# Cross-attention scores of one token tile by four row tiles into four PSUM banks, and a new order of the steps around them

## The chip, the cores and the metric

The kernel runs on one core of one Trainium2 chip. The metric is the device time of one execution in microseconds (us). A measurement of this kernel tells a change of about 1% from none.

## The reference, cut to what matters

The reference is one decoder layer on 2 x 1024 tokens of 256 values: causal self-attention with 16 heads of 16, cross-attention on 64 context rows, and a mixture of 16 experts (top 4) with a shared expert, each followed by an added residual and a layer norm. The change is in the cross-attention:

```python
q = split_heads(queries @ Wq + bq)
k = split_heads(keys @ Wk + bk)
v = split_heads(values @ Wv + bv)
scores = jnp.einsum('bhqd,bhkd->bhqk', q, k) / jnp.sqrt(jnp.float32(HD))
scores = jnp.where(mask, jnp.float32(-1000000000000000.0), scores)
attn = jax.nn.softmax(scores, axis=-1)
ctx = jnp.einsum('bhqk,bhkd->bhqd', attn, v)
...
return ctx @ Wo + bo
```

Here `HD` is 16 and there are 16 heads, so one token has 16 x 64 scores. A tile of 128 tokens has 128 x 1024 scores, which is two PSUM banks of 512 columns.

## The kernel before, in words

The program has three long stretches: the self-attention (to about 300 us of the profiled span), the cross-attention with the routing to experts (354 us to about 517 us), and 79 blocks of expert work (to about 690 us). The change touches the second.

The 2048 tokens are 16 tiles of 128. `x_order()` writes out a list `XO` of (kind, n) from the table `LAGS`, and every engine walks through this one list in its order and does the kinds that it has work for. A **step** is one pass over the table; two steps make one token tile, because kinds S, T and V come once for each half of the heads (n = 2 x tile + half). A kind with lag k handles in step s the index n = s - k. Kinds whose n must be odd come once in two steps. The kinds are:

- S: TensorE multiplies queries and keys of 8 heads into a bank and adds the mask through an identity matrix (L1643, L1645). VectorE takes the maximum over each head (L1239) and subtracts it (L1243, semaphore `xs_sub`). ScalarE takes the exponential (L833, `xp_exp`).
- T: TensorE turns the probabilities by four 128x128 transposes (L1652), ScalarE copies them out of PSUM (L840, `xpT_kept`).
- V: TensorE multiplies them with the values (L1662, `xo_ready`). The value matrix has a column of ones, so that the row sums come along.
- N, once per tile: VectorE takes the reciprocal of the sums (L1252) and scales (L1254, `xo_norm`).
- P and O: TensorE turns the context (L1672), ScalarE copies it (L846, `xo_kept`).
- Y: TensorE multiplies by the output weights (L1679, `y_ready`); VectorE adds the residual and makes the statistics of the layer norm (`norm_stats`, L990 to L996), GpSimd takes the power (L708).
- Z and X: the norm is applied by VectorE (L1039) and ScalarE (L850), TensorE turns the tile back (L1545), ScalarE copies it (L854).
- L, R, Q, W, K, I: once for each group of four tiles, the router. After I, GpSimd scatters the rows of the group to the experts' slots, 16 indirect DMAs of kind C (L738), three in a step.

All engines but TensorE's weight loads keep strictly to this order. In PSUM, banks 0 and 1 hold the scores of an even and an odd n, banks 2 and 3 the transposes of an even and an odd n, bank 4 the values of all 16 heads, bank 5 the turned context and the router's ranks, bank 6 the output product, bank 7 the turned tile and the router's logits. An S needs the subtraction two n back, a T the copy two n back.

## Time and profile before

| what | value |
|---|---|
| median of 3 runs | 711.37 us (708.14 to 714.35) |
| the profiled execution's own time | 716.99 us |
| its span in the trace | 715.3 us |
| TensorE busy over the span | 610.7 us (85%) |
| VectorE busy over the span | 469.3 us (66%) |
| ScalarE, GpSimd busy | 351.5 us (49%), 316.6 us (44%) |
| first and last score matmul (L1643) | 354.5 us, 457.8 us |

Busy is time in which an engine has an instruction in it. TensorE's matmuls overlap in the pipeline, so the time from one matmul's start to the next one's start, not the duration of one, is what it costs the engine.

### The profile page before, as it was taken

To read this page: it belongs to the slowest core of one execution; us is meant where nothing else is said; L and a number is where in the kernel's file an instruction comes from. 1 tells how busy PE (TensorE), PEld (TensorE's weight loads), DVE (VectorE), ACT (ScalarE), POOL (GpSimd) and SP (SyncE) were. 2 spreads that over 40 slices of the span, in tenths; PEclk is the share of its full clock that TensorE was granted. 3 is DMA by queue.
4 is the path that set the end of the run, shared out by engine and by line. 5 is a ranking of instruction groups with operands and counts; after the bars stand their busy time and mean duration, and the time that the engine had idled before them with its cause. 6 is when DMAs were issued, how large, how long until landed. Compare 5 with 4: busy or idle time off the path is not lost.

```text
span 715.3 us, 12852 instructions
## 1 busy us (share of the span) xinstructions
PE 610.7 (85%) x3820; PEld 369.4 (52%) x3820; DVE 469.3 (66%) x1304; ACT 351.5 (49%) x735; POOL 316.6 (44%) x393
## 2 busy tenths in 40 slices
PE   5888899999999998998799997958646888888884
PEld 3434434434434342254377774834436777777741
DVE  0369878888788883069478874736325756767657
ACT  1312376666676667816375442413223545555543
POOL 8413312234332442547666163545474454554530
PEclk9989999999999999999999996979867999999988
DMA  5867766337165300049000021111354664566756
GB/s 165 169 169 148 159 211 93 67 50 99 30 80 81 44 4 18 18 146 372 1 1 0 1 73 56 64 64 57 120 160 142 201 203 138 152 208 198 240 200 212
DMA packets 52113, 82.51 MB, mean 115 GB/s; under 512 B 11936, under 2 KB 29600, under 8 KB 51744
## 3 DMA queue, kind: packets, MB, share of 16 engines
q1 hardware_dynamic: 45184, 62.26, 35.6%
q0 software_dynamic: 6864, 19.44, 7.4%
q8 instruction: 34, 0.56, 0.3%
q14 instruction: 31, 0.25, 0.1%
HBM read 53.38 MB, written 32.48 MB: 120 GB/s over the span
## 4 chain that ended last, share of the span: by engine, by line
PE 62%; DVE 17%; another core or an unknown queue 6%; ACT 4%; issue 4%; DMA 3%; POOL 2%; SPq 1%; DVEq 0%; ACTq 0%; POOLq 0%
PE ps L1480 9%; PE ps L1745 9%; PE ps L1456 8%; PE ps L1439 7%; DVE neg_max L922 5%; PE ps L1768 4%; PE ps L1643 3%; PE ps L1662 3%; PE ps L1724 2%; PE ps L1788 2%; PE ps L1757 2%; PE ps L1588 2%; PE ps L1444 2%; PE ps L1652 2%
## 5 line engine op out<-in xcount | busy, mean ns | idle before, releaser
L922 DVE TENSOR_REDUCE neg_max<-ps 128x1 f32<-128x512 f32 (+3 forms) x304 | 181.9, 655 | 43.1 <-PE ps L1444 26.6
L775 ACT ACTIVATE temps<-ps 128x1024 f32<-128x1024 f32 (+1 forms) x192 | 147.5, 812 | 78.1 <-PE ps L1456 78.0
L674 POOL TENSOR_SCALAR_AFFINE_SELECT temps<-temps 128x256 f32<-128x256 f32 x128 | 52.2, 411 | 148.1 <-ACT temps L775 147.2
L1439 PE MATMUL ps<-stacks 96*128 96x512 bf16 (+3 forms) x384 | 105.4, 331 | 11.6 <-DMA stacks<-qk_parts 5.1
L745 POOL DMA_INDIRECT expert_outputs<-x_T,w_o_xqkv x79 | 76.6, 970 | 74.3 <-ACT x_T L895 37.5
L1456 PE MATMUL ps<-stacks 99*128 99x512 bf16 (+3 forms) x384 | 93.3, 328 | 2.9 <-DMA stacks<-m_rows 1.4
L1480 PE MATMUL ps<-temps,v_group 128*32 128x512 f32 (+3 forms) x768 | 81.8, 497 | 1.6 <-POOL temps L674 1.0
L1745 PE MATMUL ps<-w_split,block_x 128*128 x474 | 73.0, 291 | 5.8 <-DVE block_x L1327 2.9
L738 POOL DMA_INDIRECT expert_slots<-x_tok,w_o_xqkv x64 | 62.4, 974 | 28.7 <-issue 17.2
L1745 PEld LDWEIGHTS ps<-w_split,block_x 128*128 128x128 f32 x474 | 64.2, 196 | 7.4 <-issue 7.2
L1456 PEld LDWEIGHTS ps<-stacks 99*128 99x128 bf16 x384 | 26.9, 97 | 75.1 <-ACT temps L775 49.6
L1439 PEld LDWEIGHTS ps<-stacks 96*128 96x128 bf16 x384 | 37.3, 98 | 49.2 <-DVE neg_max L922 20.7
L882 ACT ACTIVATE o_norm<-ps 128x128 f32<-128x128 f32 x79 | 22.4, 283 | 60.9 <-PE ps L1745 45.0
L708 POOL TENSOR_TENSOR ln_rstd<-ln_var_eps,minus_half 128x1 f32<-128x1 f32 x32 | 18.8, 588 | 73.8 <-DVE ln_var_eps L996 73.8
L1349 DVE TENSOR_TENSOR o_norm<-ps,o_norm 128x128 f32<-128x128 f32 x79 | 22.6, 286 | 43.7 <-ACT o_norm L882 33.2
L1444 PE MATMUL ps<-caus_a,ident_b 128*128 128x128 bf16 x256 | 50.7, 224 | 0.0
L1768 PE MATMUL ps<-w_split,block_h 128*128 x237 | 50.0, 320 | 0.1
L1757 PE MATMUL ps<-ident_f,o_norm 128*128 128x128 f32 x79 | 23.7, 300 | 29.6 <-DVE o_norm L1349 20.7
L833 ACT ACTIVATE o_norm<-o_norm 128x512 f32<-128x512 f32 x32 | 20.2, 630 | 48.4 <-DVE o_norm L1243 45.7
L1327 DVE TENSOR_TENSOR block_x<-ps,block_x 128x256 fp32r<-128x256 f32 x79 | 33.1, 420 | 11.1 <-ACT block_x L874 6.5
L1494 PE MATMUL ps<-x_T,w_qkv 128*128 128x512 f32 x64 | 32.0, 642 | 7.5 <-DMA x_T<-in_xT 7.5
L874 ACT ACTIVATE block_x<-ps 128x256 fp32r<-128x256 f32 x79 | 31.0, 392 | 14.2 <-PE ps L1724 10.4
(213 smaller groups left out, 1092.6 us busy)
## 6 DMA issues: line engine op xcount, KB each, us to landing
stacks<-qk_parts SPq DMA_DIRECT2D x96, 128.0 KB, 5.7
v_group<-expert_slots SPq DMA_DIRECT2D x79, 138.5 KB
qk_parts<-temps SPq DMA_DIRECT2D x8, 768.0 KB, 4.4
w_raw<-in_w SPq DMA_DIRECT2D x4, 1024.0 KB, 10.4
early_parts<-expert_outputs SPq DMA_DIRECT2D x4, 1024.0 KB
expert_slots<-in_pad SPq DMA_DIRECT2D x16, 138.5 KB
expert_slots<-in_pad SPq DMA_DIRECT2D x1, 2077.5 KB
x_T<-in_xT SPq DMA_DIRECT2D x4, 512.0 KB, 7.4
```

Of the source, the lines that this page charges most:

```text
L674: nc.gpsimd.affine_select(diag, diag, [[0, 2], [1, P]], ALU.is_ge, zero, base=0, channel_multiplier=-1).then_inc(b_cut, 1)
L738: pool.indirect_dma_start(slots, bass.IndirectOffsetOnAxis(ridx[:, t, k:k + 1].bitcast(U32), 0), xe[:, t, :], None).then_inc(scattered[q], 16)
L745: pool.indirect_dma_start(sums_of, bass.IndirectOffsetOnAxis(idxs[:, b:b + 1].bitcast(U32), 0), yb[:, b % YB, :], None).then_inc(landed[b ...
L775: nc.scalar.activation(pt[:, n % 4, :, 0:w], ps[:, 2 + 2 * (n % 2):4 + 2 * (n % 2), 0:w], ACT.Exp, scale=SCALE).then_inc(b_exp, 1)
L922: nc.vector.tensor_reduce(nmx[:, c, h0:h0 + nh, i], ps[:, A_BANKS[n % 3], 0:w * nh].rearrange("p (h k) -> p h k", h=nh), axis=AX.X, op=ALU ...
L1439: last = nc.tensor.matmul(ps[:, A_BANKS[n % 3], w * s:w * s + w], qs[0:KR, ua, h0 + s, P * i:P * i + P], ks[0:KR, ua, h0 + s, CH * c:CH * ...
L1444: last = nc.tensor.matmul(ps[:, A_BANKS[n % 3], w * (s + 1) - P:w * (s + 1)], identb[:], causA[:], start=False, stop=True)
L1456: last = nc.tensor.matmul(ps[:, bank, 0:w], ks[0:KM, u, 2 * pr + s, P * j:P * j + P], qs[0:KM, u, 2 * pr + s, q0:q0 + w], start=True, stop ...
L1480: last = nc.tensor.matmul(ps[HS * h:HS * h + HS, 6, CH - w:CH], vg[:, u, j, h, :], pt[:, (2 * p + h // 2) % 4, h % 2, 0:w], start=(j == 0) ...
L1745: last = nc.tensor.matmul(ps[:, 2 + b % 2, 0:D], xsp[b % 3][:, xp, k, :], w13s[:, bass.ds(expert[b], 1), wp, at:at + 2 * INTER], start=(k ...
L1757: nc.tensor.transpose(ps[:, 4 + b % 2, 0:P], hblk[:, b % 3, :], identf[:]).then_inc(hb_T, 1)
L1768: last = nc.tensor.matmul(ps[:, 6 + b % 2, 0:D], hsp[:, b % 3, hp, :], w2s[:, bass.ds(expert[b], 1), wp, :], start=(n == 0), stop=(n == 2))
```

## The change

Scores: instead of one product of 128 query rows with a block-diagonal key matrix for each half of the heads, the S of an even n makes the scores of the whole tile, and the S of an odd n makes nothing on TensorE. Each group of 32 rows of the array (two heads) is a tile of its own with 128 key columns, and its scores go to bank q. Four mask matmuls of 256 columns replace two of 512. All four score banks are taken by one token tile, so that the S of an even n waits for both subtractions of the tile before. Transposes keep one bank (4), so that each T waits for the copy of the T before. The values of the two halves go to banks 5 and 6, behind columns 0 to 255. Kind Y now stands ahead of V in the table; its work on VectorE stays where it was and is now kind F.

```diff
-LAGS = {"S": 0, "T": 2, "V": 4, "N": 4, "P": 5, "O": 5, "Y": 6, "Z": 7, "X": 8, "L": 9, "R": 9, "Q": 10,
+LAGS = {"S": 0, "T": 2, "Y": 6, "V": 4, "N": 4, "P": 5, "O": 5, "F": 6, "Z": 7, "X": 8, "L": 9, "R": 9, "Q": 10,
         "W": 11, "K": 12, "I": 12}
...
-                    nc.scalar.activation(pTx[:, n % 2].rearrange("p r s -> p (r s)"), ps[:, 2 + n % 2, :],
+                    nc.scalar.activation(pTx[:, n % 2].rearrange("p r s -> p (r s)"), ps[:, 4, :],
...
                 if kind == "S":
-                    s3 = ps[:, n % 2, :].rearrange("p (h k) -> p h k", h=8)
-                    dve.wait_ge(xs_ready, n + 1)
-                    nc.vector.tensor_reduce(mxx[:, n % 2, :], s3, axis=AX.X, op=ALU.max).then_inc(xs_max, 1)
+                    s4 = ps[:, 0:4, P * (n % 2):P * (n % 2) + P].rearrange("p q (h k) -> p q h k", h=2)
+                    m3 = mxx[:, n % 2, :].rearrange("p (q h) -> p q h", h=2)
+                    dve.wait_ge(xs_ready, n // 2 + 1)
+                    nc.vector.tensor_reduce(m3, s4, axis=AX.X, op=ALU.max).then_inc(xs_max, 1)
...
                 if kind == "N":
-                    heads = ps[:, 4, 0:H * VW].rearrange("p (h v) -> p h v", h=H)
+                    heads = ps[:, 5:7, D:D + H // 2 * VW].rearrange("p o (h v) -> p o h v", v=VW)
                     dve.wait_ge(xo_ready, 2 * n + 2)
+                    wait(dve, xo_kept, n)
...
-                if kind == "Y":
+                if kind == "F":
                     dve.wait_ge(y_ready, NT + n + 1)
...
                 if kind == "S":
-                    t, o = n // 2, n % 2
-                    if n >= 2:
-                        pe.wait_ge(xs_sub, n - 1)
-                    nc.tensor.matmul(ps[:, n % 2, :], q2[:, o, P * t:P * t + P],
-                                     kbd[:, o, t // TB].rearrange("p h k -> p (h k)"), start=True, stop=False)
-                    nc.tensor.matmul(ps[:, n % 2, :], identb[:], mask[:, t, :].unsqueeze(1).to_broadcast([P, 8, S2]),
-                                     start=False, stop=True).then_inc(xs_ready, 1)
+                    if n % 2 == 0:
+                        t = n // 2
+                        wait(pe, xs_sub, n)
+                        for o in range(2):
+                            for q in range(4):
+                                rows = slice(32 * q, 32 * q + 32)
+                                nc.tensor.matmul(ps[:, q, P * o:P * o + P], q2[rows, o, P * t:P * t + P],
+                                                 kbd[rows, o, t // TB, 2 * q:2 * q + 2].rearrange("p h k -> p (h k)"),
+                                                 start=(o == 0), stop=False, skip_group_check=True)
+                        for q in range(4):
+                            last = nc.tensor.matmul(ps[:, q, 0:2 * P], identb[:],
+                                                    mask[:, t, :].unsqueeze(1).to_broadcast([P, 4, S2]),
+                                                    start=False, stop=True, skip_group_check=True)
+                        last.then_inc(xs_ready, 1)
                 if kind == "T":
                     pe.wait_ge(xp_exp, n + 1)
-                    if n >= 2:
-                        pe.wait_ge(xpT_kept, n - 1)
+                    wait(pe, xpT_kept, n)
...
                     pe.wait_ge(xpT_kept, n + 1)
-                    if o == 0 and t >= 1:
-                        pe.wait_ge(xo_norm, t)
+                    if o == 0:
+                        wait(pe, xo_norm, t)
+                        wait(pe, xo_kept, oT_turned[0])
+                        wait(pe, r_index, ranked[0])
+                    else:
+                        taken[0] = t + 1
```

TensorE's order for one token tile of the steady stretch before the change is this (v_group is the key or value matrix, o_norm the queries, probabilities or context, according to the line):

```order
L1643 MATMUL ps<-v_group,o_norm 128x512
L1645 MATMUL ps<-w_qkv,ident_b 128x512
L1652 MATMUL ps<-ident_f,o_norm 128x128 x4
L1662 MATMUL ps<-v_group,o_norm 128x34 x4
L1672 MATMUL ps<-ident_f,o_norm 128x128 x2
L1643 MATMUL ps<-v_group,o_norm 128x512
L1645 MATMUL ps<-w_qkv,ident_b 128x512
L1652 MATMUL ps<-ident_f,o_norm 128x128 x4
L1662 MATMUL ps<-v_group,o_norm 128x34 x4
L1679 MATMUL ps<-w_xo,o_norm 128x256 x2
L1545 MATMUL ps<-ident_f,x_tok 128x128 x2
```

After the change TensorE's order for one token tile of the same stretch is this:

```order
L1650 MATMUL ps<-v_group,o_norm 128x128 x8
L1654 MATMUL ps<-w_qkv,ident_b 128x256 x4
L1662 MATMUL ps<-ident_f,o_norm 128x128 x4
L1676 MATMUL ps<-v_group,o_norm 128x34 x4
L1686 MATMUL ps<-ident_f,o_norm 128x128 x2
L1662 MATMUL ps<-ident_f,o_norm 128x128 x4
L1693 MATMUL ps<-w_xo,o_norm 128x256 x2
L1676 MATMUL ps<-v_group,o_norm 128x34 x4
L1550 MATMUL ps<-ident_f,x_tok 128x128 x2
```

The scores have moved to the front of the tile as one piece, no score work stands between the first P (L1686) and the second T (L1662), and the output product Y (L1693) now stands ahead of the second V (L1676).

VectorE's order for one token tile after the change, with what each instruction waits for, is this:

```order
L1241 TENSOR_REDUCE x_max<-ps 128x8 [waits xs_ready]
L1245 TENSOR_TENSOR o_norm<-ps,x_max 128x512 [waits xp_exp,xs_max]
L1040 SCALAR_TENSOR_TENSOR ln_minus_mean<-ln_mean_var,ln_rstd 128x1 [waits ln_pow]
L1241 TENSOR_REDUCE x_max<-ps 128x8 [waits xs_ready]
L1245 TENSOR_TENSOR o_norm<-ps,x_max 128x512 [waits xp_exp,xs_max]
L1256 RECIPROCAL x_rsum<-ps 128x16 [waits xo_norm,xoT_ready,xo_kept,xo_ready]
L1258 TENSOR_TENSOR o_norm<-ps,x_rsum 128x256 [waits xo_recip]
L991 TENSOR_TENSOR x_tok<-ps,x_tok 128x256 [waits ln_done,bo_added,y_ready]
L993 BN_STATS ln_stats<-x_tok 128x6 [waits ln_in]
L995 BN_AGGR ln_mean_var<-ln_stats 128x2 [waits ln_chain]
L997 TENSOR_SCALAR ln_var_eps<-ln_mean_var 128x1 [waits ln_chain]
```

Before the change VectorE had the same instructions in the same order; only the wait for `xo_kept` ahead of the reciprocal is new. ScalarE's order is unchanged too.

## Rows read from the trace of the kernel before

**Rows 1.** The page's busy time of each engine.
```profile
PE 610.7 (85%) x3820; PEld 369.4 (52%) x3820; DVE 469.3 (66%) x1304; ACT 351.5 (49%) x735; POOL 316.6 (44%) x393
```

**Rows 2.** Timeline of TensorE, one tile: start us, us, engine, line, operation, [idle before].
```profile
383.27 1.02 PE L1643 MATMUL ps<-v_group,o_norm 128*128 128x512 f32 x2
384.13 0.38 PE L1645 MATMUL ps<-w_qkv,ident_b 128*128 128x512 bf16 x1
384.34 0.60 PE L1652 MATMUL ps<-ident_f,o_norm 128*128 128x128 f32 x4
384.78 0.98 PE L1662 MATMUL ps<-v_group,o_norm 128*128 128x34 f32 x8
385.59 0.41 PE L1672 MATMUL ps<-ident_f,o_norm 128*128 128x128 f32 x2
...
388.17 1.11 PE L1679 MATMUL ps<-w_xo,o_norm 128*128 128x256 f32 x4
389.12 0.38 PE L1545 MATMUL ps<-ident_f,x_tok 128*128 128x128 f32 x2
389.33 1.02 PE L1643 MATMUL ps<-v_group,o_norm 128*128 128x512 f32 x2
```

**Rows 3.** Timeline of VectorE and ScalarE in the same tile.
```profile
384.54 0.69 DVE L1239 TENSOR_REDUCE x_max<-ps 128x8 f32<-128x512 f32 x1
385.27 0.69 DVE L1243 TENSOR_TENSOR o_norm<-ps,x_max 128x512 f32<-128x512 f32 x1
...
386.00 0.63 ACT L833 ACTIVATE o_norm<-o_norm 128x512 f32<-128x512 f32 x1 [2.10 <-DVE o_norm L1243]
...
386.53 0.58 ACT L840 ACTIVATE o_norm<-ps 128x512 f32<-128x512 f32 x1
...
388.45 0.25 DVE L1252 RECIPROCAL x_rsum<-ps 128x16 f32<-128x16 f32 x1
...
388.74 0.42 DVE L1254 TENSOR_TENSOR o_norm<-ps,x_rsum 128x256 f32<-128x256 f32 x1
...
389.32 0.42 DVE L990 TENSOR_TENSOR x_tok<-ps,x_tok 128x256 f32<-128x256 f32 x1 [0.16 <-PE ps L1679]
...
389.78 0.43 DVE L992 BATCH_NORM_STATS2 ln_stats<-x_tok 128x6 f32<-128x256 f32 x1
...
390.45 0.15 DVE L996 TENSOR_SCALAR ln_var_eps<-ln_mean_var 128x1 f32<-128x1 f32 x1
390.61 0.69 DVE L1239 TENSOR_REDUCE x_max<-ps 128x8 f32<-128x512 f32 x1
```

**Rows 4.** Timeline of TensorE, scores of the first three tiles.
```profile
354.51 1.10 PE L1643 MATMUL ps<-v_group,o_norm 128*128 128x512 f32 x2 [0.98 <-ACT o_norm L814]
...
357.34 1.13 PE L1643 MATMUL ps<-v_group,o_norm 128*128 128x512 f32 x2 [0.44 <-DVE o_norm L1243]
...
360.47 1.02 PE L1643 MATMUL ps<-v_group,o_norm 128*128 128x512 f32 x2
```

**Rows 5.** Timeline of TensorE, self-attention products on four column tiles of 32.
```profile
120.48 0.43 PE L1480 MATMUL ps<-temps,v_group 128*32 128x128 f32 x8
...
122.70 1.06 PE L1480 MATMUL ps<-temps,v_group 128*32 128x512 f32 x8
```

**Rows 6.** Timeline: first scatter of two groups, and the ScalarE instruction after the stall.
```profile
414.42 1.20 POOL L738 DMA_INDIRECT expert_slots<-x_tok,w_o_xqkv  x1 [0.67 <-DVE w_o_xqkv L1107]
...
437.48 0.22 ACT L860 ACTIVATE w_o_xqkv<-ps 128x64 f32<-128x64 f32 x1 [5.79 <-remote]
...
451.49 1.04 POOL L738 DMA_INDIRECT expert_slots<-x_tok,w_o_xqkv  x1 [0.83 <-DVE w_o_xqkv L1107]
...
473.86 0.22 ACT L860 ACTIVATE w_o_xqkv<-ps 128x64 f32<-128x64 f32 x1 [6.50 <-remote]
```

**Rows 7.** Windows: us, busy PE, PEld, DVE, ACT, POOL, granted clock, DMA, GB/s.
```profile
588.00:595.00 7.00, 5.77 (x46) 5.30 (x45) 3.94 (x16) 3.32 (x14) 3.13 (x4) 1.00 0.53 162
```

**Rows 8.** Timeline of TensorE, values product at the lower clock.
```profile
441.29 1.76 PE L1662 MATMUL ps<-v_group,o_norm 128*128 128x34 f32 x8
```

More of the change, by code:

```diff
@@ L162, in x_order @@
                     out.append((kind, n))
-            elif kind in "NPOYZX":
+            elif kind in "NPOYFZX":
                 if n % 2 and 0 < n < 2 * NT:
@@ L563, in _ @@
             sp.wait_ge(kv_kept, 20)
-            sp.wait_ge(xs_ready, 2 * NT)
+            sp.wait_ge(xs_ready, NT)
             sp.wait_ge(bo_added, NT)
@@ L1251, in _ @@
                         dve.wait_ge(xoT_ready, n - 1)
-                    nc.vector.reciprocal(rsx[:, n % 2, :], heads[:, :, DH]).then_inc(xo_recip, 1)
+                    sums = rsx[:, n % 2, :].rearrange("p (o h) -> p o h", o=2)
+                    nc.vector.reciprocal(sums, heads[:, :, :, DH]).then_inc(xo_recip, 1)
                     dve.wait_ge(xo_recip, n + 1)
-                    nc.vector.tensor_tensor(ox[:, n % 2, :].rearrange("p (h v) -> p h v", h=H), heads[:, :, 0:DH],
-                                            rsx[:, n % 2, :].unsqueeze(2).to_broadcast([P, H, DH]),
+                    nc.vector.tensor_tensor(ox[:, n % 2, :].rearrange("p (o h v) -> p o h v", o=2, v=DH),
+                                            heads[:, :, :, 0:DH],
+                                            sums.unsqueeze(3).to_broadcast([P, 2, H // 2, DH]),
                                             ALU.mult).then_inc(xo_norm, 1)
-                if kind == "Y":
+                if kind == "F":
                     dve.wait_ge(y_ready, NT + n + 1)
@@ L1575, in project @@
             def project(c, part):
-                if c < 2 and part == 0:
-                    pe.wait_ge(xs_sub, 2 * NT - 1 + c)
-                if c < 2 and part == 1:
-                    pe.wait_ge(xpT_kept, 2 * NT - 1 + c)
+                if c < 2:
+                    pe.wait_ge(xs_sub, 2 * NT)
                 if c >= 2:
@@ L1611, in ranks @@
                 pe.wait_ge(xo_kept, oT_turned[0])
+                pe.wait_ge(xo_norm, taken[0])
                 if q >= EARLY:
@@ L1626, in ranks @@
                 if q >= 1:
-                    last = nc.tensor.matmul(ps[:, 5, D + GMAX * E:D + (GMAX + 1) * E], ones, msum[:, q], start=True,
+                    last = nc.tensor.matmul(ps[:, 5, RANK + GMAX * E:RANK + (GMAX + 1) * E], ones, msum[:, q], start=True,
                                             stop=True)
@@ L1639, in _ @@
                 if kind == "S":
-                    t, o = n // 2, n % 2
-                    if n >= 2:
-                        pe.wait_ge(xs_sub, n - 1)
-                    nc.tensor.matmul(ps[:, n % 2, :], q2[:, o, P * t:P * t + P],
-                                     kbd[:, o, t // TB].rearrange("p h k -> p (h k)"), start=True, stop=False)
-                    nc.tensor.matmul(ps[:, n % 2, :], identb[:], mask[:, t, :].unsqueeze(1).to_broadcast([P, 8, S2]),
-                                     start=False, stop=True).then_inc(xs_ready, 1)
+                    if n % 2 == 0:
[12 more added lines that the diff above has]
+                        last.then_inc(xs_ready, 1)
                 if kind == "T":
                     pe.wait_ge(xp_exp, n + 1)
-                    if n >= 2:
-                        pe.wait_ge(xpT_kept, n - 1)
+                    wait(pe, xpT_kept, n)
                     for r in range(4):
-                        last = nc.tensor.transpose(ps[:, 2 + n % 2, P * r:P * r + P], px[:, n % 2, P * r:P * r + P],
+                        last = nc.tensor.transpose(ps[:, 4, P * r:P * r + P], px[:, n % 2, P * r:P * r + P],
                                                    identf[:])
@@ L1657, in _ @@
                     pe.wait_ge(xpT_kept, n + 1)
-                    if o == 0 and t >= 1:
-                        pe.wait_ge(xo_norm, t)
+                    if o == 0:
[4 more added lines that the diff above has]
+                        taken[0] = t + 1
                     for r in range(4):
-                        at = 2 * VW * (4 * o + r)
-                        last = nc.tensor.matmul(ps[:, 4, at:at + 2 * VW], pTx[:, n % 2, r, :],
+                        at = D + 2 * VW * r
+                        last = nc.tensor.matmul(ps[:, 5 + o, at:at + 2 * VW], pTx[:, n % 2, r, :],
                                                 vbd[:, t // TB, 4 * o + r, :], start=True, stop=True)
@@ L1753, in _ @@
                     elif b == 0:
-                        pe.wait_ge(xo_norm, NT)
+                        pe.wait_ge(xpT_kept, 2 * NT)
                     else:
```

13 lines of the change are left out of this document (7 added, 6 removed).

## The prediction

> **What bounds the kernel now.** I began with the busy shares of the page, where TensorE stands first with 85% [rows 1]. A share over the whole span says little on one stage, so I went to the timeline of TensorE in the cross-attention. There a token tile costs 389.33 - 383.27 = 6.06 us from one even score product to the next, and each row of TensorE begins where the one before it lets go: two halves of scores 0.86, mask 0.21, transposes 0.44, values 0.81, P 0.25, Y 0.95, X 0.21 [rows 2]. That is 2 x (0.86 + 0.21 + 0.44 + 0.81) + 0.25 + 0.95 + 0.21 = 6.05 us with no gap. So in the steady stretch TensorE is full, and the others wait for it: VectorE's F stood 0.16 us for Y, and ScalarE 2.10 us for the subtraction [rows 3]. The reader should see a second thing in the same rows. ScalarE took the exponential at 386.00, right behind the subtraction, and only then the copy of a transpose that TensorE had finished at 384.94 [rows 2, 3]. In list order the copy of T(n-2) stands behind the exponential of S(n). Before the change this lateness costs nothing, since TensorE has a second transpose bank and a second score product to do meanwhile.
>
> **What it removes from TensorE.** A row tile of 32 appears nowhere in this trace; the nearest rows are the products on four column tiles of 32. Eight of them with 128 columns take 0.43 us together, 0.27 to issue and 0.16 to drain [rows 5]; one after another they would need 8 x 0.11, by the transposes' 0.44 for four [rows 2]. Both halves of the new scores are 16 such instructions in the trace (two passes of f32 each), so 2 x 0.27 plus a drain of 0.16 ahead of the masks, which stand in the full array; the masks are 4 x 256 columns, as many as before, 0.43, and the last ends 0.17 later. The scores of a tile are then ready 1.30 us after they start. Upper bounds: one after another 16 x 0.11 + 0.16 + 0.43 + 0.17 = 2.5; with every weight load exposed too, at the 0.10 us a load that the eight value products show [rows 2], 4.1. Lower bound 1.1, without the drain. I take 1.30, for rows 5 overlap fully and differ only in which side of the array is split. TensorE's work in a tile falls from 6.05 to 3.91 + 1.2 = 5.1 us.
>
> **What it adds: waits, in a ring.** Three things move at once. The second T of a tile waits for the copy of the first, which on ScalarE stands behind the exponential of the first half. Y stands ahead of the second V. And the second V is what N on VectorE waits for, with F and the next tile's maximum queued behind N. Followed from VectorE's first maximum of a tile: maximum and subtraction 1.42 (384.54 to 385.96), handover 0.04, exponential until the copy may start 0.53, copy 0.58 (to 387.11) [rows 3], handover to TensorE 0.05, second T 0.44, Y 0.95, second V until its end 0.98 [rows 2], handover 0.03, then N and F 390.61 - 388.45 - 0.16 = 2.00 until the next maximum may start [rows 3]. The sum is 1.42 + 0.04 + 0.53 + 0.58 + 0.05 + 0.44 + 0.95 + 0.98 + 0.03 + 2.00 = **7.02 us a tile**, against 6.06 now: +0.96. TensorE's own side of the ring, from scores ready to scores ready, is 1.42 + 0.04 + 0.53 + 0.58 + 0.05 + 0.44 + 0.95 + 0.81 + 0.21 + 1.30 = 6.33, so it is not what ends last; it would be if the scores took over 2.0 us. What is behind the waiting T on TensorE is Y, V, X and the next scores, and all of VectorE's N and F wait with them. The wait of N for `xo_kept` costs nothing: that copy is of the tile before and lies some 2 us earlier. The waits of the even V lie on copies a tile old, and the wait of SyncE is now for half the count with the same end; the two new waits at the shared expert and at the first expert block are for work long done. All of this is zero. VectorE's operands over two or four banks have as many elements as before, and I take 0.69 us [rows 3] for each.
>
> **The sum over the stretch.** Start: with one set of score banks the next scores wait for both subtractions, 1.30 + 2 x 1.42 + 0.1 = 4.24 us a tile, where the first two tiles now take 2.83 and 3.13 [rows 4]: +2.5. From there to the first scatter are 8 tiles, 8 x 0.96 = 7.7, less 0.7 for those in which the pipeline is not yet full: the first scatter starts 9.5 us later. From the first scatter of a group to the router's next ScalarE instruction pass 23.06 and 22.37 us, far more than 2.5 tiles need, with ScalarE idle for 5.79 and 6.50 us before it [rows 6]. These stretches go by the scatter's pace, and I let them hide half of 2.5 x 0.96: +1.2 each. Between them 1.5 tiles: +1.4. Behind the second, with the last score work done, +0.5. Together 9.5 + 1.2 + 1.4 + 1.2 + 0.5 = **+13.8 us**. The routing tables and the expert blocks hang on this chain and start that much later; nothing in them changes. On the profiled execution's own time that is 716.99 + 13.8 = 730.8; that execution lies 5.6 us above the median of the runs, and against the median 711.37 it is 725.2. I forecast 725 us. A 1% step, 7.1 us, is about what a measurement of this kernel can tell from no change.
>
> **Rivals.**
> (a) The row tiles don't run side by side, so the change doesn't do what it says. For it: no row of this trace shows a row tile, and 16 weight loads of 128 columns must find room where 4 did. Against it: rows 5. With 2.5 us the ring through TensorE is 5.03 + 2.5 = 7.53, +1.47 a tile. Start +4.9, 8 tiles +11.8 less 0.8, then 1.8 + 2.2 + 1.8 + 0.6: +22, 734 us. With exposed loads, 4.1 us, the tile takes 9.1 and the kernel some 42 us more, 753.
> (b) Faster, by one mechanism: the ring does not close. If the copy, Y or N of one tile could run beside the members that I put behind them, only engine work would be left, 5.1 us on TensorE, with VectorE at 2 x 1.42 + 2.00 = 4.84 beside it [rows 3]. Then 11.5 tiles gain 0.96 each, less the 2.5 of the start: -8.5, 703 us. It decides at 6.06: of the 7.02 some 0.96 would have to go, as much as Y alone. All its members stand in program order on their engines or wait by semaphore, which leaves it little. The Trainium skill, TensorEngine Tiling (Array Packing), section PSUM Bottleneck, names the copies out of PSUM as what may bound once TensorE is four times faster; read as busy time, that is this case, a gain up to VectorE's bound, while the rows above speak for the order of the waits and a loss.
> (c) The stalls of rows 6 fall elsewhere. ScalarE's 5.79 and 6.50 us wait for something that no engine releases, while indirect DMAs run. If one of them lies under other waits in the slower kernel, some 6 us come back: 719; with both, 713.
> (d) The clock. TensorE would be busy 5.1 of 7.02 us with a gap of some 2 us in each tile. A window with 5.77 of 7 busy has the clock at 1.00 throughout [rows 7]. At half the clock the values product takes 1.76 instead of 0.98 [rows 2, 8], so T, Y and V would add 1.9 us to the ring. If half of the tiles ran so, +13 more: 738. The Trainium skill, TensorE: Matmul & The Clock Gate, section A second HAM failure mode, tells of short idle times between groups of matmuls that make the clock fall back and forth; by that rule this rival would be the likely one, by rows 7 it is not.
>
> **How the numbers follow.** The ring with overlapping row tiles 0.62 (718 to 732 us, for the start, the hidden share and the drain are each uncertain by a few us), (a) 0.15 at 734 and 0.03 at 753, (c) 0.10 at 713 to 719, (d) 0.05 at 738, (b) 0.05 at 703. The range reaches from 715, which takes in the upper half of (c), to 737, which takes in the cheaper (a); left out are (b), the lower part of (c), (d) and the dear end of (a), under 2 in 10. Over 1% slower means above 718.5: all of (a) and (d), nearly all of the first, a little of (c), 0.85. Within 1%: 0.10. Faster: 0.05.
>
> **What would show it.** The score groups of 128x128 should stand with their eight entries a half in about 0.4 us, and the masks end 1.3 us after the first score. TensorE should be idle for some 1 to 2 us ahead of the second T of each tile, released by ScalarE's copy. VectorE should be idle ahead of the reciprocal, released by the values product. Even score products should stand 7.0 us apart between the tiles 5 and 9, and the first scatter should start near 9.5 us later against the first score. The distance from first scatter to the next router instruction should be near 23 to 25 us. The forecast is wrong if the distance of the tiles is under 6.1 us (the ring does not close) or over 7.5 us with long score groups (the row tiles don't overlap).

## The result, and the profile after

The changed kernel took 734.64 us (median of 4 runs, 733.30 to 745.80), the kernel before 712.86 us beside it (median of 4, 708.14 to 719.04). The ratio is **1.032, 95% interval 1.025 to 1.040**, or +23 us (+17.5 to +28.4). An execution over 1.5% above the fastest of its kernel goes into no ratio in this document, here 745.80 and 719.04 us. The profiled execution took 733.3 us with a span of 731.6, 16.3 above the span of before.

The page, busy times and the clock over 40 slices, against [rows 1]:

```profile
PE 612.7 (84%) x4044; PEld 383.2 (52%) x4044; DVE 469.1 (64%) x1304; ACT 353.6 (48%) x735; POOL 317.7 (43%) x393
...
PEclk9989899999999999999759978697975999999998
```

The clock row of before:

```profile
PEclk9989999999999999999999996979867999999988
```

The busy times are within 14 us of what they were, and say nothing of where 16 us went. The clock rows say something. In the stretch that the change touches, digits of 5 to 8 now begin with the twentieth slice (348 us); before they began with the twenty-fifth (429 us), behind the first scatter.

TensorE's timeline over one steady tile, against [rows 2]:

```profile
390.22 0.73 PE L1650 MATMUL ps<-v_group,o_norm 32*128 32x128 f32 x16
390.88 0.61 PE L1654 MATMUL ps<-w_qkv,ident_b 128*128 128x256 bf16 x4
391.33 0.60 PE L1662 MATMUL ps<-ident_f,o_norm 128*128 128x128 f32 x4
391.76 0.98 PE L1676 MATMUL ps<-v_group,o_norm 128*128 128x34 f32 x8
392.58 0.42 PE L1686 MATMUL ps<-ident_f,o_norm 128*128 128x128 f32 x2
394.61 0.63 PE L1662 MATMUL ps<-ident_f,o_norm 128*128 128x128 f32 x4 [1.62 <-ACT o_norm L841]
395.07 1.03 PE L1693 MATMUL ps<-w_xo,o_norm 128*128 128x256 f32 x4
395.94 0.98 PE L1676 MATMUL ps<-v_group,o_norm 128*128 128x34 f32 x8
396.75 0.42 PE L1550 MATMUL ps<-ident_f,x_tok 128*128 128x128 f32 x2
397.10 0.73 PE L1650 MATMUL ps<-v_group,o_norm 32*128 32x128 f32 x16
```

A tile takes 397.10 - 390.22 = 6.88 us. From the first of the sixteen products on row tiles to the next row pass 0.66 us, so they overlap. The second T waits 1.62 us for ScalarE's copy (L841).

VectorE and ScalarE in the same tile, against [rows 3]:

```profile
391.91 0.68 DVE L1241 TENSOR_REDUCE x_max<-ps 128x8 f32<-128x512 f32 x1
392.62 0.69 DVE L1245 TENSOR_TENSOR o_norm<-ps,x_max 128x512 f32<-128x512 f32 x1
...
396.95 0.26 DVE L1256 RECIPROCAL x_rsum<-ps 128x16 f32<-128x16 f32 x1 [1.79 <-PE ps L1676]
...
398.94 0.68 DVE L1241 TENSOR_REDUCE x_max<-ps 128x8 f32<-128x512 f32 x1
```
```profile
393.35 0.63 ACT L834 ACTIVATE o_norm<-o_norm 128x512 f32<-128x512 f32 x1 [2.34 <-DVE o_norm L1245]
393.89 0.58 ACT L841 ACTIVATE o_norm<-ps 128x512 f32<-128x512 f32 x1
```

Here is the ring, link by link: maximum at 391.91, subtraction, exponential at 393.35, copy at 393.89, second T at 394.61, Y, second V at 395.94, reciprocal at 396.95, maximum of the next tile at 398.94.

The same in the waits view of 356 to 490 us (total, times, longest):

```profile
ACT o_norm L834 <- DVE o_norm L1245: 55.6, 21, 6.3
DVE x_rsum L1256 <- PE ps L1676: 27.7, 12, 4.8
PE ps L1662 <- ACT o_norm L841: 22.8, 14, 5.2
```

Three engines wait for one another in a circle, and none of them is full.

The scores of the first tiles, against [rows 4], with two waits of transposes:

```profile
356.96 0.73 PE L1650 MATMUL ps<-v_group,o_norm 32*128 32x128 f32 x16 [0.98 <-ACT o_norm L815]
...
361.06 0.73 PE L1650 MATMUL ps<-v_group,o_norm 32*128 32x128 f32 x16 [2.83 <-DVE o_norm L1245]
...
365.33 1.09 PE L1662 MATMUL ps<-ident_f,o_norm 128*128 128x128 f32 x4 [1.89 <-ACT o_norm L841]
366.35 1.24 PE L1650 MATMUL ps<-v_group,o_norm 32*128 32x128 f32 x16
...
424.45 1.08 PE L1662 MATMUL ps<-ident_f,o_norm 128*128 128x128 f32 x4 [2.75 <-ACT o_norm L841]
```

The second tile comes 4.10 us behind the first (4.24 in the sum). In the third tile, and in the two behind it, the same sixteen products take 1.24 us instead of 0.73: that is the clock. Windows of the start (us, busy PE, PEld, DVE, ACT, POOL, granted clock, DMA, GB/s):

```profile
361.00:368.00 7.00, 5.04 (x47) 3.79 (x48) 2.68 (x5) 4.06 (x9) 7.00 (x9) 0.57 0.00 0
...
375.00:382.00 7.00, 6.64 (x29) 5.91 (x28) 2.67 (x4) 2.96 (x6) 0.00 (x0) 0.50 0.01 2
382.00:389.00 7.00, 6.23 (x46) 5.46 (x47) 4.83 (x11) 3.01 (x6) 3.84 (x5) 0.73 0.00 0
389.00:396.00 7.00, 5.38 (x56) 4.72 (x54) 4.88 (x11) 3.47 (x8) 3.66 (x5) 1.00 0.01 2
...
424.00:431.00 7.00, 6.12 (x39) 5.29 (x39) 4.90 (x17) 2.57 (x6) 0.18 (x1) 0.50 0.00 0
```

A 0.50 is TensorE at 1.2 GHz, a 1.00 at 2.4. Behind the 2.83 us of waiting ahead of the second tile the engine is low for most of 28 us. A busy share read alone would mislead here: 6.64 of 7 us busy, since each instruction lasts longer. In the steady tiles of this trace, with a gap of 1.62 to 1.77 us in each, the clock is full. From 424 us on, behind a wait of 2.75 us, it is at 0.50 again.

The scatters and the router, against [rows 6]:

```profile
432.04 1.20 POOL L739 DMA_INDIRECT expert_slots<-x_tok,w_o_xqkv  x1 [0.67 <-DVE w_o_xqkv L1108]
...
457.29 0.22 ACT L861 ACTIVATE w_o_xqkv<-ps 128x64 f32<-128x64 f32 x1 [2.09 <-remote]
...
473.57 1.04 POOL L739 DMA_INDIRECT expert_slots<-x_tok,w_o_xqkv  x1 [0.83 <-DVE w_o_xqkv L1108]
...
494.23 0.22 ACT L861 ACTIVATE w_o_xqkv<-ps 128x64 f32<-128x64 f32 x1 [3.47 <-remote]
```

Cut at the first scores and the first scatter of each of the four groups, the two executions differ so: first scores +2.5 us, to the first scatter 75.1 instead of 59.9 (+15.2), to the second 41.5 instead of 37.1 (+4.4), to the third +2.2, to the fourth +0.2, from there to the end -8.2. Of the last piece 4.5 us lie among the 79 expert blocks (from the first to the last scatter of their outputs 145.3 us before and 140.9 here), which the change leaves as they were, and 3.3 us behind them, where TensorE's granted clock was 0.79 before (687 to 701 us) and 1.00 here (711 to 717 us). ScalarE's waits that no engine releases lie elsewhere, between the scatters: 5.79 and 6.50 us ahead of the router's instruction in [rows 6], 2.09 and 3.47 here. With the other waits of that kind between the same scatters they come to 10.7 and 11.3 us before, 7.5 and 8.4 here. The execution of before was 5.6 us above the median of the runs that the forecast went by, that of after 1.3 below its own.

### The profile page after: what moved, and what is told of

It is laid out like the page before. It is cut to its first block, busy times and chain, and to the rows that moved or that the text cites. A ratio compares the mean times of both kernels' runs of the same rounds, so it can differ in the third digit from the quotient of the medians.

```text
span 731.6 us, 13325 instructions
## 1 busy us (share of the span) xinstructions
PE 612.7 (84%) x4044; PEld 383.2 (52%) x4044; DVE 469.1 (64%) x1304; ACT 353.6 (48%) x735; POOL 317.7 (43%) x393
## 3 DMA queue, kind: packets, MB, share of 16 engines
q1 hardware_dynamic: 45184, 62.26, 34.8%
## 4 chain that ended last, share of the span: by engine, by line
PE 54%; DVE 19%; DMA 6%; issue 6%; ACT 5%; another core or an unknown queue 4%; POOL 2%; SPq 2%; DVEq 0%; ACTq 0%; POOLq 0%
PE ps L1485 9%; PE ps L1461 8%; PE ps L1444 7%; PE ps L1759 7%; DVE neg_max L923 5%; PE ps L1782 3%; PE ps L1676 2%; DMA v_group<-expert_slots 2%; PE ps L1693 2%; PE ps L1738 2%; PE ps L1449 2%; PE ps L1591 2%; DVE x_max L1241 2%; PE ps L1662 2%
## 5 line engine op out<-in xcount | busy, mean ns | idle before, releaser
L1444 PE MATMUL ps<-stacks 96*128 96x512 bf16 (+3 forms) x384 | 106.8, 336 | 10.7 <-DMA stacks<-qk_parts 4.9
L739 POOL DMA_INDIRECT expert_slots<-x_tok,w_o_xqkv x64 | 62.3, 974 | 28.7 <-issue 17.2
L883 ACT ACTIVATE o_norm<-ps 128x128 f32<-128x128 f32 x79 | 22.3, 282 | 53.7 <-PE ps L1759 37.4
L1662 PE MATMUL ps<-ident_f,o_norm 128*128 128x128 f32 x128 | 24.9, 328 | 23.6 <-ACT o_norm L841 22.8
L1771 PE MATMUL ps<-ident_f,o_norm 128*128 128x128 f32 x79 | 23.6, 299 | 22.7 <-DVE o_norm L1354 19.4
L1676 PEld LDWEIGHTS ps<-v_group,o_norm 128*128 128x128 f32 x256 | 39.2, 227 | 6.0 <-ACT o_norm L841 4.7
L1676 PE MATMUL ps<-v_group,o_norm 128*128 128x34 f32 x256 | 37.4, 297 | 4.5 <-ACT o_norm L841 4.5
```

Source lines behind the costliest of these rows:

```text
L739: pool.indirect_dma_start(slots, bass.IndirectOffsetOnAxis(ridx[:, t, k:k + 1].bitcast(U32), 0), xe[:, t, :], None).then_inc(scattered[q], 16)
L1444: last = nc.tensor.matmul(ps[:, A_BANKS[n % 3], w * s:w * s + w], qs[0:KR, ua, h0 + s, P * i:P * i + P], ks[0:KR, ua, h0 + s, CH * c:CH * ...
L1676: last = nc.tensor.matmul(ps[:, 5 + o, at:at + 2 * VW], pTx[:, n % 2, r, :], vbd[:, t // TB, 4 * o + r, :], start=True, stop=True)
```

## The experiments

They ran in groups on several chips, each beside the kernel before on the same chip. In three groups the kernel before takes 656 to 658 us, in the other two groups, the result's and the last, 710 to 713. So only differences and ratios are compared. "Stretches" are the times from the first scores to the first scatter, and from scatter to scatter.

### The changed kernel and the kernel before on a quicker chip

Both unmodified.

> The changed kernel, unmodified, beside the three that follow on one chip. The ring theory (a tile of a tail lasts 6.88 us against 6.06, and the clock falls while the pipeline fills) does not lean on the long idle stretches of the first trace: the steps are the same on any chip, so the difference in us stays, +18 to +24 over the kernel before, and the granted clock is again 0.5 to 0.75 in the first 30 us behind the first scores. The rival, that part of the difference came from where those idle stretches fall, gives less than +14 on a chip where they are absent.

> The kernel before, unmodified, for its trace on the kind of chip where it takes some 656 us. A steady tile 6.06 us, the sixth tile's scores 22.7 us behind the first, and the first scatter about 60 us behind, all as in the first trace, since none of this leans on where it ran. The rival, that the tails themselves differ from chip to chip, gives other values for these three.

Measured: changed kernel 684.98 us median (677.51 to 689.40, 4 runs) beside 657.67, profiled at 681.63 with a span of 679.7. Of the four, 677.51 and 681.63 us count for a ratio, which is about 1.034. Before, on another chip of the quicker kind: 658.77 us, span 657.0. The difference of the spans is 22.7 us. In the trace of before a tile is 6.07 us, the sixth tile comes 22.7 us behind the first, the first scatter 59.9: the tails are the same on both kinds of chip. For the changed kernel these are 6.88 (one tile, from 386.85 us), 32.2 and 77.4. Windows of the changed kernel from its first scores on, and then of before:

```profile
354.00:390.00 36.00, 25.90 (x228) 22.04 (x228) 18.92 (x38) 15.64 (x32) 17.97 (x25) 0.81 0.00 1
390.00:432.00 42.00, 34.62 (x268) 29.96 (x269) 27.64 (x86) 17.00 (x36) 11.53 (x16) 0.77 0.01 2
```
```profile
354.00:377.00 23.00, 22.57 (x125) 15.38 (x126) 17.09 (x32) 14.48 (x30) 15.99 (x21) 1.00 0.01 1
377.00:414.00 37.00, 35.27 (x228) 27.11 (x227) 30.52 (x92) 16.66 (x37) 13.03 (x19) 0.99 0.00 1
```

Here the clock fell in the steady tiles too. At 398.26 us TensorE came out of the ring's own wait, and the two tiles that begin at 393.73 and 401.98 us took 8.25 and 8.99 us:

```profile
398.26 0.63 PE L1662 MATMUL ps<-ident_f,o_norm 128*128 128x128 f32 x4 [1.76 <-ACT o_norm L841]
```
```profile
399.00:409.00 10.00, 9.64 (x54) 8.28 (x53) 5.42 (x11) 3.87 (x8) 4.24 (x6) 0.52 0.00 0
```

In the first trace the same wait, 1.77 us, ended at 401.63 us, and the clock stayed at 1.00.

The stretches differ by +17.5, +2.9, +3.3 and +1.0 us, the start by +0.7, the rest behind the last scatter by -2.8. That last piece is again the work behind the expert blocks, at a clock of 0.79 before (635 to 643 us) and 1.00 for the changed kernel (659 to 666 us). What differs between the chips is ScalarE's wait: the router's instruction (L860) has no idle time before it here.

```profile
429.86 0.20 ACT L860 ACTIVATE w_o_xqkv<-ps 128x64 f32<-128x64 f32 x1
```

So the loss does not hang on where those stalls fall. The first scores' +2.5 us of the first trace are +0.7 here and lie ahead of everything that the change touches.

### One part alone in the kernel before: Y ahead of V

```diff
-LAGS = {"S": 0, "T": 2, "V": 4, "N": 4, "P": 5, "O": 5, "Y": 6, "Z": 7, ...
+LAGS = {"S": 0, "T": 2, "Y": 6, "V": 4, "N": 4, "P": 5, "O": 5, "F": 6, "Z": 7, ...
```

> The kernel before with kind Y ahead of V in the table (its VectorE part as kind F in the old place), nothing else; banks and scores as before. My theory, the ring of waits: Y waits for ScalarE's copy O, which stands behind the exponential and the transposes' copy, and now V and with it N wait behind Y. Members by the rows of before: N and F 2.00, maximum and subtraction 1.42, exponential 0.53, copy 0.58, O 0.38, Y 0.95, V 0.98 with handovers 0.1: 6.9 us a tile instead of 6.06, so some 7 to 9 us more in all, although TensorE has all its old work. Rival: TensorE is full at 6.05 us a tile and its work is only reordered, so the time stays within 2 us of before.

Measured: 665.69 us, ratio 1.016 (1.013 to 1.019). Scores, masks and banks are those of before. The tile grew to 390.31 - 383.62 = 6.69 us (6.9 expected), with one gap:

```profile
388.28 1.13 PE L1679 MATMUL ps<-w_xo,o_norm 128*128 128x256 f32 x4 [0.41 <-ACT o_norm L846]
```

Y now waits for ScalarE's copy O (L846), and V stands behind it, though V's own data are there. The first stretch grew by 3.4 us. The clock stayed at 1.00 in every window from 353 to 460 us: the order of Y alone costs, without any help from the clock.

### One part alone in the kernel before: one bank for the transposes

```diff
-                    if n >= 2:
-                        pe.wait_ge(xpT_kept, n - 1)
+                    wait(pe, xpT_kept, n)
-    transpose(ps[:, 2 + n % 2, P * r:P * r + P], ...)
+    transpose(ps[:, 2, P * r:P * r + P], ...)
```

> The kernel before with one bank for the transposes instead of two, nothing else. Theory of the prediction, that the second T waits for the copy behind the exponential: here a score product of 1.07 us stands between, so T reaches its turn 2.57 us after the scores and the copy is done at about 2.6: 6.1 to 6.4 us a tile, and 1 to 2 us in the start; 2 to 7 us more in all. Rival: the single bank alone makes the whole loss, 7.0 us a tile and some 14 us more.

Measured: 666.49 us, ratio 1.017 (1.013 to 1.022), a tile of 6.43 us, the first stretch 65.6 instead of 59.9. The gap ahead of T is short, 0.17 us by L840, because the score products of the second half stand between the two T and cover the copy. In the changed kernel these have moved to the head of the tile. The tile is near the expected 6.1 to 6.4 us, the loss of 10.4 us is above the expected 2 to 7: the first stretch holds 5.6 of it, and where the rest lies was not found. The start of this kernel has gaps too, TensorE is busy for 3.67 us from 360 to 366 us, and there the clock stayed at 1.00. Each part alone costs about 10 us, and both together with the single set of score banks 22.7.

### The ring cut at its ScalarE link

In the changed kernel, ScalarE gets a list XA of its own, in which T (in the second kernel T and O) stands ahead of S in each step, and so the copy of the transposes ahead of the exponential:

```diff
-            for kind, n in XO:
+            for kind, n in XA:
```

> The changed kernel, but ScalarE does the copy of the transposes ahead of the exponential in each step. Theory: exponential and copy leave the ring at the second T; what is left is the ring through O and Y, without the copy: 6.3 us a tile instead of 6.88, so 5 to 8 us less than the changed kernel. Rival: the clock or VectorE decides, and the time stays within 2 us of the changed kernel. Second rival: the exponentials come later by the copy and the tile gets longer.

> The changed kernel, but ScalarE does both the copy of the transposes and the copy O of the turned context ahead of the exponential. Theory: both rings through ScalarE open, and TensorE's 5.1 us, VectorE's 4.9 us and what is left of handovers decide: 5.4 to 5.8 us a tile, 10 to 14 us less than the changed kernel, about the time of the kernel before (the start still costs 2 to 9 us). Rival: as for the run with the copy alone ahead, if O is no member, 6.3 us a tile.

Measured: copy ahead 675.46 us, ratio 1.033 (1.026 to 1.040), tile 6.21 to 6.36 us. Copy and O ahead 669.37 us, ratio 1.023 (1.015 to 1.030), tile 5.85 us. TensorE in the second of them:

```profile
386.52 0.63 PE L1663 MATMUL ps<-ident_f,o_norm 128*128 128x128 f32 x4 [0.59 <-ACT o_norm L842]
```

The wait of the second T fell from 1.62 to 0.59 us and the tile by 1.03, below the 6.07 of before. The link is shown. The times followed less well than the tiles. With the copy alone ahead the ratio is that of the changed kernel (1.032 and about 1.034), where 5 to 8 us less were expected, and with both copies the kernel is still 2% slower than before, where about the time of before was expected: what is left of the loss does not lie in the steady tile. In the window from 360 to 366 us its clock was 0.50.

### The same order on ScalarE in the kernel before

XA has T and O ahead of S again.

```diff
-            for kind, n in XO:
+            for kind, n in XA:
```

> The kernel before with ScalarE's copy of the transposes and O ahead of the exponentials, which took 1.03 us off a tile of the changed kernel. With two banks for the transposes and two for the scores no ring closes through ScalarE there, and VectorE's and TensorE's rows set the tile: 6.0 us, the same time within 2 us. The rival, that the order on ScalarE was costing the kernel before as well, gives a tile below 5.9 and 3 to 8 us less.

Measured: 657.36 us beside 656.67, ratio 1.001 (0.997 to 1.005), tile 6.07 us. Where two banks hide the lateness of the copy, its place in the list is worth nothing that shows. No version came out ahead of the kernel before.

### A member of the ring made shorter

```diff
-                    for o in range(2):
+                    for o in range(1):
                         last = nc.tensor.matmul(ps[:, 6, 0:D], oTx[:, n % 2, o, :], wxo[:, o, :], ...
```

> The changed kernel with one of the two matmuls of each output projection Y left out, so half of the attention's heads do not reach the result. This shortens Y by about half of its 0.95 us. If Y lies on the ring of waits, a steady tile shrinks from 6.88 to 6.4 or 6.5 us and the time by 6 to 9 us; if the ring closes beside Y, as the rival has it, TensorE idles longer where Y was, and both stay.

Measured: **686.20 us beside 656.67, ratio 1.045** (1.037 to 1.054). The tile shrank as expected, to 6.54 us on the average of four (378.68 to 404.85): Y is on the ring. The first stretch shrank too, from 77.4 us on the quicker chip to 70.7. The time did not; with less to do for TensorE the kernel is no faster than the changed one, in the ratio even above its 1.032. The windows of the second and the third stretch:

```profile
424.00:462.00 38.00, 36.47 (x226) 31.64 (x225) 22.79 (x77) 13.85 (x29) 18.24 (x21) 0.54 0.17 61
462.00:500.00 38.00, 35.77 (x165) 29.47 (x164) 17.26 (x67) 12.55 (x25) 18.10 (x21) 0.57 0.18 61
```

The second and third stretch last 37.4 and 37.9 us, 4.5 and 7.4 more than in the changed kernel on the quicker chip, at a clock of 0.54 and 0.57 where that one had 0.93 and 0.89. That was the first hint that in this kernel the clock can outweigh the ring. Over the whole span all four executions have a lower granted clock, 0.913 to 0.921, than any of the changed kernel's on the quicker chip, 0.935 to 0.954. Why it fell is not shown, and in time two of the changed kernel's executions, 688.33 and 689.40 us, lie where these four do (685.17 to 689.85).

### The row tiles taken away

```diff
-                                rows = slice(32 * q, 32 * q + 32)
+                                rows = slice(0, P)
```

> The changed kernel with each score matmul over all 128 rows of the array (the rows of the other heads of kbd are zeros, so the result is the same): sixteen matmuls can no longer run four at a time. Sixteen by about 0.11 us, a fill of 0.43 and a handover of 0.17 make scores ready about 2.3 us after their start instead of 1.27. If the scores lie on the ring, a steady tile lasts about 7.3 to 7.9 us instead of 6.88, and the time is 7 to 20 us above the changed kernel's; that would also say what the row tiles themselves save. The rival, that the ring closes without the scores, gives a tile of 6.88 again and a time within 2 us.

Measured: 682.85 us, ratio 1.040 (1.030 to 1.050). The tile is 7.52 us, with the score products at 1.95:

```profile
386.23 1.95 PE L1650 MATMUL ps<-v_group,o_norm 128*128 128x128 f32 x16
388.01 0.60 PE L1654 MATMUL ps<-w_qkv,ident_b 128*128 128x256 bf16 x4
...
391.36 0.63 PE L1662 MATMUL ps<-ident_f,o_norm 128*128 128x128 f32 x4 [1.25 <-ACT o_norm L841]
```

So the row tiles save 0.64 us a tile. Scores are ready after 388.01 - 386.23 + 0.60 = 2.38 us here (the masks start at 388.01), and the ring on TensorE's side, which the prediction put at 5.03 us without the scores, gives 7.41: with long scores that is the ring that ends last. The first stretch is 76.7 us against 77.4 with row tiles, and the time is near that of the changed kernel on the same chip: 681.48 to 683.59 us in the three executions that count, against 677.51 and 681.63, where 7 to 20 us more were expected. The gain of the row tiles in the tile does not show in the first stretch, and the windows of this kernel show one reason:

```profile
352.00:387.00 35.00, 25.62 (x201) 24.23 (x202) 16.83 (x32) 14.91 (x30) 16.30 (x21) 0.95 0.00 1
387.00:429.00 42.00, 34.99 (x296) 32.92 (x295) 30.99 (x92) 16.90 (x37) 12.86 (x19) 1.00 0.00 1
```

0.95 and 1.00, where the changed kernel has 0.81 and 0.77 on the same chip. Longer products on TensorE, and in the steady tiles shorter gaps (1.25 us), went with a higher clock. At the start its gaps are no shorter, 2.83, 2.31 and 1.50 us against the changed kernel's 2.83, 1.89 and less, and yet the clock was low only from 362 to 366 us (0.59). So the length of the gaps alone does not decide.

### The gaps filled

Matmuls of no use into a bank that is free at that moment, in TensorE's waits only. First at the start of the tails, in the changed kernel and in the one with copy and O ahead:

```diff
+            filled_for = {("S", 2): 13, ("T", 1): 8, ("T", 3): 5, ("T", 5): 2}
             for kind, n in XO:
+                for _ in range(filled_for.get((kind, n), 0)):
+                    nc.tensor.matmul(ps[:, 7, :], identb[:], mask[:, 0:8, :]..., start=True, stop=True)
```

> The changed kernel with matmuls of no use (128 by 512, into the bank that is unused) in TensorE's idle stretches of the first tiles of each stage: 13 ahead of the scores of the second tile, 8, 5 and 2 ahead of three sets of transposes. If the low granted clock of the start is what makes the sixth tile come 33.3 us behind the first instead of about 28, the clock stays near 1.00 there, the sixth tile comes 28 to 29 us behind, and the time is 3 to 6 us below the changed kernel's. The rival, that the start is slow by its waits alone, gives the same 33 us or more and a time that is the same or up to 3 us longer.

> The same filling matmuls in the kernel whose ScalarE takes the copy of the transposes and O ahead of the exponentials. Its tile is 5.85 us already, below the 6.06 of before, but its clock fell in the start too. If the clock is what is left of the loss there, it gains about 4 us on that kernel, and comes to a ratio of 1.01 to 1.02 over before; a steady tile stays 5.85. The rival, that what is left of the loss lies behind the tails (later scatters, the router's wait), leaves it at 1.023 whatever the clock does.

Measured, changed kernel with filling: 677.51 us (675.06 to 679.10), ratio 1.031 (1.023 to 1.039), and without it 677.51 and 681.63 us in the two executions that count on the same chip. The window from the first to the sixth tile:

```profile
352.00:380.00 28.00, 23.75 (x223) 17.79 (x226) 15.96 (x30) 14.36 (x29) 16.00 (x21) 1.00 0.00 1
```

The sixth tile's scores come 28.0 us behind the first instead of 32.2 (33.3 in the first trace), and the first stretch is 69.2 us instead of 77.4. Of these 8.2 us the second and third stretch give back 5.6 (35.3 and 33.8 instead of 32.9 and 30.5), at a clock of 0.79 and 0.77 instead of 0.93 and 0.89. Between the profiled executions 4.1 us of span remain, in which the first scores alone, ahead of any filling, come 2.7 us earlier; what the filling is worth to the whole kernel is therefore not settled by this run, what it does to the start is.

Copy and O ahead with filling: 663.63 us, ratio **1.009** (1.005 to 1.013), against 1.023 without, on another chip of the same kind. Its first stretch is 61.0 us instead of 65.5, its tile 5.85 as before. Of the 5.6 us that this stretch was above the 59.9 of before, 4.5 went with the filling: there the clock was most of what was left.

Then in the changed kernel in all its long waits, from T 7 on in bank 6, which F of the tile before must have read:

```diff
+            filled_for = {("S", 2): 13, ("T", 1): 8, ("T", 3): 5, ("T", 5): 2, ("T", 7): 6, ("T", 9): 6, ("T", 11): 6,
+                          ("T", 13): 6, ("T", 17): 12, ("T", 19): 5, ("T", 21): 4, ("T", 25): 12, ("T", 27): 3,
+                          ("T", 29): 6}
...
+                if filler and kind == "T" and n > 5:
+                    wait(pe, ln_in, NT + projected)
```

> The changed kernel with matmuls of no use in all of TensorE's longer idle stretches of the tails: at the start as in e7_fill_start, and then 3 to 12 ahead of ten further sets of transposes, where the traces of the changed kernel show 0.6 to 2.8 us of waiting. This is the changed kernel as the forecast's sum had it, ring and all, with the clock taken out. If the sum was right and only the clock was missing in it, a steady tile stays 6.88 us, the granted clock is at or near 1.00 from the first scores to the last scatter, the first scatter comes 69 to 70 us behind the first scores, the next two steps between scatters last 31 to 32.5 us instead of 35.3 and 33.8, and the time is 12 to 16 us over the kernel before, 669 to 673 us here. If the forecast's terms themselves were too small, the clock is up and the time stays 18 us or more over; if the added matmuls only delay what waits behind them, the tile grows past 7.1 us.

Measured: 726.72 us beside 709.88, ratio 1.022 (1.017 to 1.028): **+15.9 us (+12.1 to +19.7)**. This chip is of the slower kind, so the 669 to 673 us of the expectation are read as the 12 to 16 us over before from which they came. TensorE in one tile, the filling at L1651:

```profile
388.48 0.73 PE L1662 MATMUL ps<-v_group,o_norm 32*128 32x128 f32 x16
...
391.09 1.46 PE L1651 MATMUL ps<-w_qkv,ident_b 128*128 128x512 bf16 x6
393.01 0.63 PE L1674 MATMUL ps<-ident_f,o_norm 128*128 128x128 f32 x4 [0.47 <-ACT o_norm L841]
...
395.50 0.73 PE L1662 MATMUL ps<-v_group,o_norm 32*128 32x128 f32 x16
```

```profile
354.00:382.00 28.00, 25.21 (x236) 18.34 (x235) 16.28 (x31) 14.74 (x29) 15.68 (x20) 1.00 0.01 2
382.00:422.00 40.00, 36.59 (x335) 29.22 (x331) 30.13 (x94) 17.18 (x38) 13.05 (x19) 1.00 0.01 1
```

The tiles are 6.88 and 7.02 us in turn, the filling delays nothing, the clock is 1.00 up to the first scatter, and this comes 68.2 us behind the first scores. Behind it the expectation does not hold: the next two stretches last 38.9 and 36.5 us, at a clock of 0.91 and 0.82. This is a chip with the stalls of [rows 6], where before has 37.1 and 34.8; the expected 31 to 32.5 were those of a chip without them. Against 37.1 and 34.8 these stretches are 1.8 and 1.7 us longer.

## Why the prediction was right, and where its size was off

**The ring.** 7.02 us a tile were summed, 6.88 stand in the trace (7.02 in one of the three behind 390.22). All its members are there, in the order in which they were added. That it is a ring was shown by changing its members: the transposes' copy ahead of the exponential took 0.52 to 0.67 us off the tile, both copies ahead 1.03, half of Y 0.34 on the average, and longer scores put 0.64 on it.

**The row tiles.** Scores ready after 1.30 us was the forecast, 1.27 the measurement. Rival (a), that they do not overlap, is out: 0.66 us from the first of sixteen to the next row, 1.78 where the full array was used. The Trainium skill, TensorEngine Tiling (Array Packing), section PSUM Bottleneck, says that the copies out of PSUM may bound next. The trace agrees in that a copy ends TensorE's wait, and disagrees with a reading by busy time: VectorE and ScalarE are not full, the copy is late in its list.

**The stretches behind the first scatter.** +1.2, +1.4, +1.2 and +0.5 were taken, 4.3 in all. Measured +4.4, +2.2 and +0.2 in the first trace and +2.9, +3.3 and +1.0 on the quicker chip, so 6.8 and 7.2. The two terms of +1.2 stood for the way from the first scatter of a group to the router's next ScalarE instruction, half of a delay of 2.4 us being hidden. In the first trace this way lasts 25.3 and 20.7 us instead of 23.1 and 22.4, so +2.2 and -1.7, and on the quicker chip 17.2 and 18.3 instead of 16.1 and 14.5, so +1.2 and +3.8. A fixed half is not what is hidden there; what sets the share is open.

**The term that was mis-sized** is "the first scatter starts 9.5 us later". It was +15.2 us from the first scores on, and +17.5 on the quicker chip. With the gaps filled and the clock at 1.00 it was +8.3 (68.2 against 59.9), with the start alone filled +9.3. So the 9.5 were right for the waits, and 6 to 9 us on top (15.2 - 9.3 to 17.5 - 8.3) are the clock, which the sum had at 1.00 throughout. With them the whole comes to 13.8 + 6 to 9 = 20 to 23 us, against a measured +23 (17.5 to 28.4) and +22.7; with the clock mostly taken out the kernel measured +15.9 (12.1 to 19.7), in which 13.8 lies.

**Where luck helped.** The ring by itself was given 718 to 732 us, and 734.64 lies outside that. The range reached on to 737 to take in the cheaper (a), at 734 us, which is not what happened. And the sum of 20 to 23 meets the measured one in part because two misses cancel: the stretches behind the first scatter are 2.5 and 2.9 us longer than the sum had them, and the piece behind the last scatter, which it left unchanged, came out 8.2 and 2.8 us shorter.

**Rival (d)** was given 0.05 on the strength of [rows 7], a stretch with short gaps and a full clock. For the steady tiles that reading held in the first trace (gaps of 1.62 to 1.77 us, clock 1.00) and failed in the second, where the clock was 0.52 for 10 us behind a gap of 1.76. It was also carried over to the start, where it does not belong. There TensorE waits 2.83 us for the second subtraction, then 1.89 and 1.18 us ahead of transposes, in tiles that have no Y and few V yet. The sum had this start, at 4.24 us a tile, and did not ask what the clock does in it. So of the +13 us at which (d) stood, on top of the ring, 6 to 9 came, in the stretch up to the first scatter. The clock fell again behind a wait of 2.75 us at 421.70 us, where VectorE has a routing step in its list. The Trainium skill, TensorE: Matmul & The Clock Gate, section A second HAM failure mode, has short idle times between groups of matmuls as what makes the clock go back and forth. The traces agree for the start and behind the routing step, and for the steady tiles of the second trace; they do not for the steady tiles of the first, nor for the start of the kernel with one transpose bank, and hardly for that of the kernel with full rows. What decides between these is open.

**Rival (b)** is out with the ring. **Rival (c)** is out as a gain of the change. The stalls ahead of the router's instruction were 4 and 3 us shorter in the first trace of the changed kernel, yet the stretches that hold them grew by 4.4 and 2.2 us, and where no such stall stands, on the quicker chip, the loss is the same. The 8.2 us behind the last scatter are not shown to be of this kind: 3.3 of them go with a higher clock, and 4.5, among the expert blocks, are unexplained. Why the stalls differ from chip to chip is open.

Open too: how much of the 22 us each of the three parts carries when the others are in place. The two that were tried alone cost 1.6% and 1.7%; the single set of score banks was not tried alone.

## What to carry to other kernels

When TensorE is given shorter work or fewer banks, follow one item round the circle of engines in program order and add it up: the tile was 6.9 us though TensorE, the fullest engine, had 5.3 us of work in it (6.88 - 1.62). Then look at the fill of the pipeline by itself, and price it at both levels of the clock: with half of Y less the granted clock was lower and nothing was gained, and cheap matmuls in the gaps gave 8 us on one stretch, of which the next two took back 5.6. A double buffer that looks idle may be what hides a late copy two engines away.

## What was not expected of the hardware

- Half the Y matmuls left out: the tile 0.34 us shorter, the granted clock 0.54 and 0.57 in two stretches, and the kernel at 1.045 of before.
- Sixteen score products on the full array (1.95 us) and on row tiles (0.73 us) gave kernel times within 3 us of each other (682.4 and 679.6 on the average of the executions that count), the former at a clock of 0.95 and 1.00 in the first stretch, the latter at 0.81 and 0.77.
- The same wait of the same program, 1.77 and 1.76 us in a steady tile, left the clock at 1.00 in one execution and had it at 0.52 for 10 us behind it in another.
- The same program took 656 to 658 us in three groups of runs and 710 to 713 us in two. In the two traces of before 7.1 us of this lie between the first and the second scatter, 7.6 between the second and the third, and 40 us behind the last; on the slower chip ScalarE stands for 5.79 and 6.50 us ahead of the router's instruction with no engine releasing it, on the quicker one not at all.
